# Selective scan: the row steps also make dt, B and C of the column directions, and both row sweeps run first

## Chip, cores and metric

One core of one Trainium2 chip. The metric is the device time of one launch in microseconds; before the change it is 9641.94 us, the median of 3 runs (9639.81 to 9643.63).

## What is computed

Two layers over x of shape (8, 192, 64, 64), float32. The change is in the first, a two-dimensional selective scan over four directions (k = 0: rows, 1: columns, 2: rows backwards, 3: columns backwards). Cut to what matters:

```
xn = layernorm(x); xc, z = split(in_proj_w @ xn)
xc = silu(depthwise_conv3x3(xc) + conv_b)
x_hw = xc as (D, L), rows after each other        # L = 64 * 64 = 4096
x_wh = xc transposed, columns after each other
xs = stack([x_hw, x_wh, reversed x_hw, reversed x_wh])
dts, B, C = split(x_proj_w[k] @ xs[k], [12, 16])   # 12 + 4 + 4 rows
dt = softplus(dt_proj_w[k] @ dts + dt_proj_b[k])
h = exp(dt * A) * h + dt * B * u ; y = sum_n h[n] * C[n]
y of the four directions is summed in image order, + Ds * xs
out = x + out_proj_w @ (layernorm(y) * silu(z))
```

The second layer is an attention over the 4096 positions with a residual; the change does not touch it. dts, B and C of a position are linear in xc at that position, so they do not depend on the order in which a direction walks over the image.

## The kernel before

The batch is a loop over 8 images. In one image come four stages with a barrier of all engines between them (the first two run into each other): project and convolve, scan, mix, attend. In the profile an image takes about 1206 us, of which the scan's 32 steps take about 470.

**Steps.** `run_chunks` (line 216) unrolls 32 steps per image: direction k = 0, 1, 2, 3 in turn, and in each 8 chunks of 512 positions. An odd k reads its chunk of 8 columns out of the row-ordered tiles with a stride of 64 elements between neighbours (`chunk`, line 99). `body` of every engine gets the steps before, now, next and after (two ahead), because the work of a step is spread over three steps:

- two steps ahead, PE makes the 20 rows dts, B and C (`xdbl`, lines 408 and 409, two products over the 192 channels), ACT copies them to `xd` (line 735), PE makes dt's argument from `xd` (`dtproj`, line 416), ACT does softplus in pieces (lines 745 to 761), ACT and DVE split the same 20 rows in a high and a low part in `xhl` (`copy_high`, line 741, and `low_half`, line 1096), DVE makes the softplus residue (line 1102), and SP writes the B rows to memory (line 299) and reads them back spread over all partitions (`bs`, lines 302 and 305);
- one step ahead, DVE finishes softplus (`softplus`, line 1108), POOL makes dt + relu (line 951), dt * u (`du`, line 957, which reads a chunk of u) and three products with B (`dbu`, line 966);
- in its own step, ACT makes the decays (line 768), DVE scans six tiles (line 1118) and multiplies them by C in three instructions (line 1126), which need C spread over the partitions: PE does that (`spread`, line 427, two products in fp32r for each of q = 0, 1, 2). PE then sums y with the sum so far, which it reads back from `pad0` and `pad1` (`sum_first` line 435 and 438, `sum_second` 444, `sum_rest` 451 and 454), and ACT writes the sum back (lines 773 and 777).

**Order on each engine** is written out by hand and held by semaphores. On PE a step is xdbl of the step two ahead, sum_rest of the step before, spread 1, dtproj, sum_first, spread 2, sum_second, spread 0 of the next step. On DVE it is scans and C product three times (softplus of the next step after the first), then low_half and residue of the step two ahead. PSUM: bank 0 holds xdbl's result, 1 the sum, 2 and 3 the decays, 4 and 5 the spread C, 6 and 7 softplus.

`pad0` and `pad1` hold the padded input of the convolution in the first stage and the two parts of the sum in the scan. A list LOADS of weight transfers is issued by SP once, before the first image, and everything waits for them.

Of the kernel before, what the change touches and what calls it, by code (L numbers as in the profile page):

```python
# [19 lines left out]
F32 = mybir.dt.float32  # L20
# [6 lines left out]
L = HH * WW  # L27
# [10 lines left out]
LO = 32  # L38
PW = WW + 2
# [11 lines left out]
def build(nc, nb, x, vec, w_in, w_x, w_dt, sel, fold, ident, w_out, w_att, gb, w_w, out):  # L51
# [3 lines left out]
    with ctx:  # L55
# [6 lines left out]

        pad0 = sb("pad0", [P, PW * PW])
        pad1 = sb("pad1", [P, PW * PW])
# [15 lines left out]
        wx0 = sb("wx0", [P, K * P])  # L80
        wx1 = sb("wx1", [P, K * P])
# [15 lines left out]
        Y = [pad0, pad1]  # L97
# [71 lines left out]
        rden = nc.dram_tensor("rden", [T], F32, kind="Internal").ap()  # L169
        rows = [nc.dram_tensor(f"rows{i}", [NS, T], F32, kind="Internal").ap() for i in range(2)]  # L170
# [6 lines left out]
        def barrier(eng, b, n):  # L177
# [15 lines left out]
            "xdbl_ready", "xd_ready", "xhi_ready", "xlo_ready", "dtpre_ready", "soft_ready", "res_ready", "sp_ready",  # L193
# [11 lines left out]
        LOADS = [(vecs[:, :], vec), (wx0[:, :].rearrange("p (k n) -> p k n", n=P)[:, :, 0:64], w_x[0:P].rearrange("p (k n) -> p k n", n=64)),  # L205
                 (wx1[:, :].rearrange("p (k n) -> p k n", n=P)[:, :, 0:64], w_x[P:2 * P].rearrange("p (k n) -> p k n", n=64)),
                 (wdt[0:NX + 1, :], w_dt), (foldw[:, R:P], fold), (eye[:, :], ident), (wo0[:, R:C], w_out[0:P, 0:P]), (wo0[:, 0:R], w_out[0:P, P:C]),
                 (wo1[0:R, R:C], w_out[P:C, 0:P]), (wo1[0:R, 0:R], w_out[P:C, P:C]),
                 (wa0[:, :], w_att[0:P]), (wa1[0:R, :], w_att[P:C]), (wa1[R:R + 1, 2 * O:3 * O], gb), (ww[:, :], w_w), (gate[0:64, 0, 0:12 * P], sel)]
# [6 lines left out]
        def run_chunks(eng, b, body):  # L216


            def place(k, n):
                k, n = k + n // NCH, n % NCH  # L220
                return (k, n if k < 2 else NCH - 1 - n) if 0 <= k < K else None

            for k in range(K):
                for n in range(NCH):
                    body(k, n % 2, b * G + (k * NCH + n), place(k, n - 1), place(k, n), place(k, n + 1), place(k, n + 2))
# [45 lines left out]
        def _(sp):  # L271
            sp.wait_ge(S["pads_set"], 10)
# [14 lines left out]
            with sp.Fori(0, nb) as b:  # L287
# [8 lines left out]
                def body(k, par, g, before, now, nxt, after):  # L296
                    sp.wait_ge(S["xd_ready"], g + 1)
                    sp.wait_ge(S["dbu_ready"], g * NP + 1)
                    sp.dma_start(rows[par], xd[RANK:RANK + NS, :]).then_inc(S["rows_saved"], 16)
# [3 lines left out]
                    for half in range(2):  # L303
                        part = rows[par].rearrange("(e w) t -> w e t", w=2)[half:half + 1].to_broadcast([R, 2, T])
                        sp.dma_start(bs[par][half * R:half * R + R, 2, :, :], part).then_inc(S[f"b_loaded{par}"], 16)
                run_chunks(sp, b, body)
# [40 lines left out]
        def _(pe):  # L347
# [10 lines left out]
            with pe.Fori(0, nb) as b:  # L358
# [45 lines left out]
                def xdbl(k, c, g):  # L404

                    pe.wait_ge(S["xlo_ready"], g + 1)
                    order = k % 2
                    mm(flat(ps[:, 0, :]), wx0[:, k * P:(k + 1) * P], chunk(u[:, 0], c, order), start=True, stop=False)  # L408
                    mm(flat(ps[:, 0, :]), wx1[:, k * P:(k + 1) * P], chunk(u[:, 1], c, order), start=False, stop=True)\  # L409
                        .then_inc(S["xdbl_ready"], 1)  # L410

                def dtproj(k, g):
                    pe.wait_ge(S["xd_ready"], g + 1)
                    pe.wait_ge(S["dt_ready"], g + 1)
                    for r in range(2):
                        m = mm(ps[:, 6 + r, :], wdt[:, (2 * k + r) * P:(2 * k + r + 1) * P], xd[:, :],  # L416
                               start=True, stop=True)
# [966 lines left out]
```

## Time and profile before

| what | value |
|---|---|
| median of 3 runs | 9641.94 us |
| profiled execution: its own time | 9653.1 us |
| its span, first to last instruction | 9651.3 us |
| PE busy, of the span | 9020.4 us, 93% |
| DVE busy | 7422.2 us, 77% |
| ACT busy | 6225.7 us, 65% |
| POOL busy | 3292.1 us, 34% |
| mean granted TensorE clock | 0.974 of full speed |

Times are microseconds from the span's start unless marked ns. PE is TensorE's matmul, DVE is VectorE, ACT is ScalarE, POOL is GpSimd, SP issues the transfers. L427 is line 427 of the kernel. Busy time of PE is modelled from pipelined matmuls; what its work costs is better read from the distance between the starts of rows that follow each other without a wait. One fp32 product of 128x512 shows as two matmul records, one fp32r product as one. The times here belong to the profiled execution, 11 us above the median.

### The profile page before, as it was taken

What the parts mean: (1) busy time and instruction counts of PE and PEld (TensorE: products, weight loads), DVE (VectorE), ACT (ScalarE), POOL (GpSimd) and SP (SyncE); (2) the same over time, 40 slices, a digit from 0 to 9 for tenths busy, and PEclk for the clock granted to TensorE, in tenths of its full rate; (3) what the DMA queues carried; (4) which work ended last, traced back from release to release, by engine and by line L of the source; (5) the groups of instructions that cost most, each with busy time, mean ns of one, the idle gap of its engine ahead of it and who ended that gap; (6) DMA issues with size and microseconds to landing.
All of it is one profiled execution on the core that took longest, in us unless ns stands there. A gap on an engine that the chain in (4) does not pass through costs nothing. (4 is left out here: it accounts for less than half of the span.)

```text
span 9651.3 us, 105800 instructions
## 1 busy us (share of the span) xinstructions
PE 9020.4 (93%) x27076; PEld 4814.2 (50%) x27076; DVE 7422.2 (77%) x8305; ACT 6225.7 (65%) x7692; POOL 3292.1 (34%) x1873
## 2 busy tenths in 40 slices
PE   7999989999899998999989999899998999989999
PEld 3336733367333673336733367333663336633466
DVE  6977679776797767977679776797767977679776
ACT  6765667656675566755667556675567755677555
POOL 3850038500385003850038500384003840048400
PEclk9999999999999999999999999999999999999999
DMA  2320013200132001320013200232002320023100
GB/s 66 106 71 11 12 58 106 70 11 12 58 108 68 11 12 60 110 66 10 12 63 108 66 10 12 65 106 66 10 12 65 106 66 10 12 65 110 61 10 13
DMA packets 214540, 499.71 MB, mean 52 GB/s; under 512 B 71001, under 2 KB 71993, under 8 KB 181262
## 3 DMA queue, kind: packets, MB, share of 16 engines
q1 hardware_dynamic: 214030, 494.10, 16.8%
q8 instruction: 174, 2.85, 0.1%
q14 instruction: 336, 2.75, 0.1%
HBM read 466.39 MB, written 27.38 MB: 51 GB/s over the span
## 5 line engine op out<-in xcount | busy, mean ns | idle before, releaser
L1255 DVE TENSOR_TENSOR pl<-pf,ph 128x1024 fp32r<-128x1024 f32 x1024 | 1254.0, 1225 | 1021.9 <-ACT ph L901 1014.7
L1118 DVE TENSOR_TENSOR_SCAN h<-ps,h,dbu 128x512 f32<-128x512 f32 x1536 | 1884.2, 1267 | 50.3 <-POOL dbu L966 32.6
L966 POOL TENSOR_TENSOR dbu<-bs,du 128x1024 f32<-128x1024 f32 x768 | 1799.2, 2372 | 54.1 <-POOL du L957 54.1
L901 ACT ACTIVATE ph<-pf 128x1024 fp32r<-128x1024 f32 x1024 | 1085.7, 1060 | 758.7 <-PE ps L601 758.5
L895 ACT ACTIVATE pf<-ps 128x1024 f32<-128x1024 f32 x1024 | 1050.9, 1026 | 536.3 <-PE ps L588 536.3
L921 POOL MEMSET sqb<- 64x512 f32 x16 | 8.3, 519 | 4003.4 <-issue 3998.5
L768 ACT ACTIVATE ps<-dt,negA 128x512 f32<-128x512 f32 x1536 | 1032.5, 683 | 409.1 <-DVE h L1118 401.6
L1239 DVE TENSOR_REDUCE mx<-ps 128x1 f32<-128x512 f32 x1792 | 1167.8, 683 | 78.9 <-PE ps L506 61.2
L1126 DVE TENSOR_TENSOR hc<-h,ps 128x1024 f32<-128x1024 f32 x768 | 937.4, 1221 | 198.4 <-PE ps L427 118.5
L957 POOL TENSOR_TENSOR du<-dt,u 128x512 f32<-128x512 f32 x512 | 715.0, 1419 | 647.6 <-DVE dt L1108 646.9
L951 POOL TENSOR_TENSOR dt<-dt,ze 128x1024 f32<-128x1024 f32 x256 | 605.9, 2367 | 922.4 <-ACT dt L761 922.4
L586 PE MATMUL ps<-thc,phh 97*128 97x512 f32 x2048 | 846.0, 413 | 6.8 <-ACT thc L878 6.8
L427 PE MATMUL ps<-xhl,selr 128*128 128x512 f32 x1536 | 698.8, 536 | 148.3 <-DVE hc L1126 148.3
L599 PE MATMUL ps<-ph,gth 128*97 128x512 f32 x2048 | 818.5, 400 | 11.7 <-DVE pl L1255 8.6
L587 PE MATMUL ps<-thc,phl 97*128 97x512 f32 x2048 | 815.4, 398 | 0.0
L588 PE MATMUL ps<-thc,phh 97*128 97x512 f32 x2048 | 812.8, 397 | 0.0
L601 PE MATMUL ps<-pl,gth 128*97 128x512 f32 x2048 | 810.6, 396 | 0.0
L600 PE MATMUL ps<-ph,gtl 128*97 128x512 f32 x2048 | 809.2, 395 | 0.0
L506 PE MATMUL ps<-phh,thc 96*128 96x512 f32 x1824 | 632.7, 408 | 47.3 <-POOLq L180 18.8
L416 PE MATMUL ps<-xd,wdt 128*128 128x512 f32 x1024 | 509.2, 621 | 81.8 <-DVE dt L1108 74.7
L427 PEld LDWEIGHTS ps<-xhl,selr 128*128 128x128 f32 x1536 | 267.7, 192 | 607.4 <-DVE hc L1126 395.9
L454 PE MATMUL ps<-hc,foldw 128*128 128x512 f32 x1024 | 495.1, 606 | 0.0
(188 smaller groups left out, 15369.5 us busy)
## 6 DMA issues: line engine op xcount, KB each, us to landing
bs<-rows SPq DMA_DIRECT2D x256, 1024.0 KB, 5.2
bs<-rows SPq DMA_DIRECT2D x512, 256.0 KB, 6.1
xa<-in_x SPq DMA_DIRECT2D x130, 256.0 KB, 2.9
xb<-in_x SPq DMA_DIRECT2D x130, 128.0 KB, 3.0
out<-fa SPq DMA_DIRECT2D x64, 256.0 KB, 2.0
rdb<-rden SPq DMA_DIRECT2D x56, 192.0 KB, 3.4
out<-fa SPq DMA_DIRECT2D x64, 128.0 KB, 2.3
rows<-xd SPq DMA_DIRECT2D x256, 8.0 KB
```

The source lines that it names most:

```text
L427: m = mm(ps[:, 4 + e, :], selr[:, j * P:(j + 1) * P], xhl[par][:, :], start=True, stop=True)
L586: mm(dst, kk, thc[par][0][:, :], start=True, stop=False)
L587: mm(dst, phl[:, m * P:(m + 1) * P], thc[par][0][:, :], start=False, stop=False)
L599: mm(dst, gth[:, m, :], ph[:, mp % 2, e, :], start=(m == 0), stop=False)
L768: A(ps[:, 2 + e, :], dt[par][:, 0 if j < NS else 1, :], ACT.Exp, scale=negA[:, k * NT + j:k * NT + j + 1]).then_inc(S["dA_ready"], 1)
L895: A(pf[:, mp % 2, :, :], ps[:, 2 * (mp % 2):2 * (mp % 2) + 2, :], ACT.Exp)\
L901: A(ph[:, mp % 2, :, :], pf[:, mp % 2, :, :], ACT.Copy).then_inc(S["ph_ready"], 1)
L966: pool.tensor_tensor(dbu[:, q, :, :], bs[par][:, q, :, :], du[:, r:r + 1, :].to_broadcast([P, 2, T]), ALU.mult).then_inc(S["dbu_ready"], 1)
L1118: dve.tensor_tensor_scan(h[:, j, ::step], ps[:, 2 + e, ::step], dbu[:, q, e, ::step], h[:, j, end:end + 1], ALU.mult, ALU.add)\
L1126: TT(hc[:, q, :, :], h[:, 2 * q:2 * q + 2, :], ps[:, 4:6, :], ALU.mult).then_inc(S["hc_ready"], 1)
L1239: dve.tensor_reduce(mx[:, t, m:m + 1], ps[:, 5 + j % 2, :], AX.X, ALU.max)\
L1255: TT(pl[:, mp % 2, :, :], pf[:, mp % 2, :, :], ph[:, mp % 2, :, :].bitcast(F32), ALU.subtract)\
```

## The change

- The order of the sweeps is k = 0, 2, 1, 3, so the 16 row steps come before the 16 column steps.
- The x_proj product of a row step now has more columns of weight: besides the 20 rows of its own direction it gives C of directions 1 and 3 (in two copies, at partitions 20 to 27 and 84 to 91) and dts and B of directions 1 and 3 (from partitions 32 and 48). Time per product depends on the 512 positions, which stay.
- In 8 of the 16 row steps (STORE), which cover the 8 row chunks once, ACT also writes all of the product's result to a new tile `xsf`, transposed to column order (`store_xs`; `xsf` lies over `pad1`), and SP writes the C rows, high and low, from `xhl` to a new tensor `ct` in memory, in row order.
- Column steps have no xdbl, no copy to `xd`, no copy_high and no low_half. dtproj reads `xsf`, SP takes the B rows from `xsf`, and SP reads the C rows from `ct` into `xhl`, in pieces of 8 elements (64 rows of the image by 8 columns, for 4 partitions, two such transfers per step). `spread` then reads `xhl` with a stride of 8 elements (32 bytes), in column order.
- copy_high and low_half of the row steps cover 128 and 64 partitions instead of 64 and 32.
- The second part of the sum moves from `pad1` to `gate[:, 1]`.
- LOADS grows from 23 to 58 transfers, because the weights are put together column by column.

```diff
+ORDER = (0, 2, 1, 3)
+EV = 2 * NCH
+STORE = (3, 5, 7, 9, 11, 13, 14, 15)
+ONE = NX + 2 * NS
...
+        for w, rows_ in ((wx0, slice(0, P)), (wx1, slice(P, 2 * P))):
+            for s, k in enumerate((0, 2)):
+                at = s * P
+                LOADS += [(w[:, at:at + NX], w_x[rows_, 64 * k:64 * k + NX]), (w[:, at + R + RANK + NS:at + R + NX], w_x[rows_, 64 * k + RANK + NS:64 * k + NX])]
+                for i, kk in enumerate((1, 3)):
+                    c_of, m = w_x[rows_, 64 * kk + RANK + NS:64 * kk + NX], at + NX + NS * i
+                    LOADS += [(w[:, m:m + NS], c_of), (w[:, R + m:R + m + NS], c_of),
+                              (w[:, at + LO + 16 * i:at + LO + 16 * i + 16], w_x[rows_, 64 * kk:64 * kk + 16])]
...
@@ SP, body
+                    if at < EV:
+                        sp.wait_ge(S["xd_ready"], b * EV + (at + 1))
+                        src = xd[RANK:RANK + NS, :]
+                    else:
...
+                        src = xsf[m:m + NS, bass.ds(c * T, T)]
                     sp.wait_ge(S["dbu_ready"], g * NP + 1)
...
+                    if at in STORE:
+                        sp.wait_ge(S["xlo_ready"], b * EV + (at + 2))
+                        for m, row in ((0, NX), (2 * NS, R + NX)):
+                            sp.dma_start(ct[m:m + 2 * NS, c * T:(c + 1) * T], xhl[par][row:row + 2 * NS, :].bitcast(F32))\
+                                .then_inc(S[f"c_stored{par}"], 16)
+                    if at >= EV:
...
+                        sp.wait_ge(S["cbc_ready"], g * NP + 1)
+                        for m, row in ((0, RANK + NS), (2 * NS, R + RANK + NS)):
+                            m += NS * (k // 2)
+                            src = ct[m:m + NS, :].rearrange("r (h w) -> r h w", w=WW)[:, :, c * RPC:(c + 1) * RPC]
+                            dst = xhl[par][row:row + NS, :].bitcast(F32).rearrange("p (h w) -> p h w", w=RPC)
+                            sp.dma_start(dst, src).then_inc(S[f"c_loaded{par}"], 16)
...
@@ PE
+                    src = xd[:, :] if at < EV else xsf[:, c * T:(c + 1) * T]
...
-                        m = mm(ps[:, 4 + e, :], selr[:, j * P:(j + 1) * P], xhl[par][:, :], start=True, stop=True)
+                        src = flat(xhl[at % 2][:, :]) if at < EV else xhl[at % 2][:, :].rearrange("p (h w) -> p w h", w=RPC)
+                        m = mm(flat(ps[:, 4 + e, :]), selr[:, j * P:(j + 1) * P], src, start=True, stop=True)
...
-                    if after:
-                        xdbl(*after, g + 2)
+                    if after and at + 2 < EV:
+                        xdbl(*after, b * EV + (at + 2))
...
@@ ACT
+                def store_xs(c):
+
+                    A(chunk(xsf, c, 1), flat(ps[:, 0, :]), ACT.Identity, bias=eye[:, ONE:ONE + 1]).then_inc(S["xs_ready"], 1)
...
                         soft_exp(g + 2)
-                        copy_high(par, g + 2)
+                        if at + 2 in STORE:
+                            store_xs(after[1])
+                        if at + 2 < EV:
+                            copy_high(at + 2, g + 2)
...
@@ DVE
                     if after:
-                        low_half(par, g + 2)
+                        if at + 2 < EV:
+                            low_half(at + 2)
                         residue(g + 2)
```

How this moves instructions is seen best at two places.

PE, a column step in the middle of a sweep, before (pad is `pad1` in L451 and `pad0` in L435, hc the scanned tiles times C):

```order
L408 MATMUL ps<-u,wx 128x512 [waits xlo_ready]
L409 MATMUL ps<-u,wx 128x512
L451 MATMUL ps<-pad,eye 128x512 [waits y0_added]
L452 REGISTER_ALU
L454 MATMUL ps<-hc,foldw 128x512 [waits hc_ready]
L454 MATMUL ps<-hc,foldw 128x512
L422 REGISTER_ALU
L427 MATMUL ps<-xhl,selr 128x512 [waits hc_ready]
L427 MATMUL ps<-xhl,selr 128x512
L416 MATMUL ps<-xd,wdt 128x512 [waits dt_ready,xd_ready]
L416 MATMUL ps<-xd,wdt 128x512
```

and the same stretch of a column step now:

```order
L502 MATMUL ps<-gate,eye 128x512 [waits y0_added]
L503 REGISTER_ALU
L505 MATMUL ps<-hc,foldw 128x512 [waits hc_ready]
L505 MATMUL ps<-hc,foldw 128x512
L470 REGISTER_ALU
L478 MATMUL ps<-xhl,selr 128x512 [waits hc_ready]
L478 MATMUL ps<-xhl,selr 128x512
L462 REGISTER_ALU
L465 MATMUL ps<-xsf,wdt 128x512 [waits dt_ready]
L465 MATMUL ps<-xsf,wdt 128x512
```

The two xdbl products are gone. The rest is the same in number and order, but L478 reads `xhl` with its stride, which these rows do not show.

ACT, a row step whose chunk two ahead is stored, now (from softplus's exponential, L808, to the sum's first part, L829):

```order
L808 ACTIVATE za<-za 128x1024 [waits soft_ready]
L790 ACTIVATE xsf<-ps,eye 128x8x64
L794 ISA
L797 ACTIVATE xhl<-ps 128x512 [waits cbc_ready]
L811 REGISTER_ALU
L812 ACTIVATE ps<-za 128x1024 [waits soft_ready]
L816 REGISTER_ALU
L817 ACTIVATE dt<-za 128x1024 [waits du_ready]
L823 ISA [waits dt_ready]
L824 ACTIVATE ps<-dt,negA 128x512 [waits scan_link]
```

L790 is new, and stands ahead of copy_high (L797), softplus's last two parts and the decay (L824) that the next step's first scan waits for.

## Rows read from the trace of the kernel before

**Rows 1.** The page's part 1: busy us (share of the span) xinstructions.
```profile
PE 9020.4 (93%) x27076; PEld 4814.2 (50%) x27076; DVE 7422.2 (77%) x8305; ACT 6225.7 (65%) x7692; POOL 3292.1 (34%) x1873
```
**Rows 2.** Timeline of DVE, first scans of steps 8, 16 and 24: start, us, what.
```profile
1491.20 2.46 DVE L1118 TENSOR_TENSOR_SCAN h<-ps,h,dbu 128x512 f32<-128x512 f32 x2 [0.33 <-DVE h L1145]
...
1611.86 2.46 DVE L1118 TENSOR_TENSOR_SCAN h<-ps,h,dbu 128x512 f32<-128x512 f32 x2 [0.34 <-POOL dbu L966]
...
1727.24 2.46 DVE L1118 TENSOR_TENSOR_SCAN h<-ps,h,dbu 128x512 f32<-128x512 f32 x2 [0.33 <-DVE h L1145]
```
**Rows 3.** Timeline of DVE, the end of a row step.
```profile
1652.98 0.68 DVE L1096 TENSOR_TENSOR xhl<-ps,xhl 32x512 fp32r<-32x512 f32 x1
1653.70 1.23 DVE L1102 SCALAR_TENSOR_TENSOR ps<-ps,za 128x1024 f32<-128x1024 f32 x1
1654.96 1.28 DVE L1118 TENSOR_TENSOR_SCAN h<-ps,h,dbu 128x512 f32<-128x512 f32 x1
```
**Rows 4.** Timeline of DVE, a column step.
```profile
1520.95 2.46 DVE L1118 TENSOR_TENSOR_SCAN h<-ps,h,dbu 128x512 f32<-128x512 f32 x2
...
1524.67 1.22 DVE L1108 SCALAR_TENSOR_TENSOR dt<-ps,dt 128x1024 f32<-128x1024 f32 x1
...
1533.09 1.22 DVE L1126 TENSOR_TENSOR hc<-h,ps 128x1024 f32<-128x1024 f32 x1 [1.12 <-PE ps L427]
...
1536.32 1.28 DVE L1118 TENSOR_TENSOR_SCAN h<-ps,h,dbu 128x512 f32<-128x512 f32 x1
```
**Rows 5.** Timeline of PE, the same column step.
```profile
1521.49 1.90 PE L409 MATMUL ps<-u,wx 128*128 128x512 f32 x2
1523.21 1.90 PE L451 MATMUL ps<-pad,eye 128*128 128x512 f32 x2
1524.93 1.90 PE L454 MATMUL ps<-hc,foldw 128*128 128x512 f32 x4
...
1527.12 1.88 PE L416 MATMUL ps<-xd,wdt 128*128 128x512 f32 x4
...
1530.54 1.90 PE L438 MATMUL ps<-hc,eye 128*128 128x512 f32 x4
...
1534.36 0.73 PE L427 MATMUL ps<-xhl,selr 128*128 128x512 f32 x2
1535.08 1.96 PE L408 MATMUL ps<-u,wx 128*128 128x512 f32 x2
```
**Rows 6.** Timeline of PE, a row step.
```profile
1640.31 1.02 PE L409 MATMUL ps<-u,wx 128*128 128x512 f32 x2
1641.17 1.02 PE L451 MATMUL ps<-pad,eye 128*128 128x512 f32 x2
```
**Rows 7.** Timeline of ACT: line 773 in a column step and in a row step.
```profile
1536.55 1.03 ACT L773 ACTIVATE pad<-ps 128x512 f32<-128x512 f32 x1
...
1654.65 0.58 ACT L773 ACTIVATE pad<-ps 128x512 f32<-128x512 f32 x1
```
**Rows 8.** Timeline of POOL, a column step.
```profile
1526.06 3.03 POOL L957 TENSOR_TENSOR du<-dt,u 128x512 f32<-128x512 f32 x2 [2.72 <-DVE dt L1108]
1529.26 7.03 POOL L966 TENSOR_TENSOR dbu<-bs,du 128x1024 f32<-128x1024 f32 x3 [0.17 <-POOL du L957]
1536.25 2.36 POOL L951 TENSOR_TENSOR dt<-dt,ze 128x1024 f32<-128x1024 f32 x1
```
**Rows 9.** Timeline of ACT, the end of a row step.
```profile
1651.53 1.01 ACT L756 ACTIVATE ps<-za 128x1024 f32<-128x1024 f32 x1
...
1653.42 1.29 ACT L768 ACTIVATE ps<-dt,negA 128x512 f32<-128x512 f32 x2
```
**Rows 10.** Timeline of SP's issues, the first and the last of LOADS.
```profile
4.59 0.41 SPq L274 DMA_DIRECT2D vecs<-in_vec  x1
...
12.61 4.53 SPq L274 DMA_DIRECT2D win<-in_w_in  x8
```
**Rows 11.** DMA issues: names, engine, op, count, KB each, median us to landing.
```profile
thc<-nmr SPq DMA_DIRECT2D x224, 0.5 KB, 2.0
```

More of the change, by code:

```diff
@@ L63, in build @@
         pad0 = sb("pad0", [P, PW * PW])
+        with ExitStack() as at_pad1:
+            xsf = sb("xsf", [P, L], where=at_pad1)
         pad1 = sb("pad1", [P, PW * PW])
@@ L216, in run_chunks, with place @@
         def run_chunks(eng, b, body):
[L219 to L225, printed above, removed]
+            def place(at):
+                if not 0 <= at < G:
+                    return None
+                k, n = ORDER[at // NCH], at % NCH
+                return k, n if k < 2 else NCH - 1 - n
+            for at in range(G):
+                body(at, at % 2, b * G + at, place(at - 1), place(at), place(at + 1), place(at + 2))
         def run_project(eng, step, early=None):
@@ L271, in _ @@
         def _(sp):
[L272 removed]
+            sp.wait_ge(S["pads_set"], 11)
             for dst, src in LOADS:
@@ L294, in _, with body @@
                 sp.sem_inc(mark, 1)
-                def body(k, par, g, before, now, nxt, after):
-                    sp.wait_ge(S["xd_ready"], g + 1)
+                def body(at, par, g, before, now, nxt, after):
+                    k, c = now
+                    if at < EV:
+                        sp.wait_ge(S["xd_ready"], b * EV + (at + 1))
+                        src = xd[RANK:RANK + NS, :]
+                    else:
+                        if at == EV:
+                            sp.wait_ge(S["xs_ready"], b * NCH + NCH)
+                        m = LO + 16 * (k // 2) + RANK
+                        src = xsf[m:m + NS, bass.ds(c * T, T)]
                     sp.wait_ge(S["dbu_ready"], g * NP + 1)
-                    sp.dma_start(rows[par], xd[RANK:RANK + NS, :]).then_inc(S["rows_saved"], 16)
+                    sp.dma_start(rows[par], src).then_inc(S["rows_saved"], 16)
                     sp.wait_ge(S["rows_saved"], g * 16 + 32)
@@ L402, in step, with xdbl @@
                         remainder(c - 2)
[L404 to L409, printed above, removed]
-                        .then_inc(S["xdbl_ready"], 1)
-                def dtproj(k, g):
-                    pe.wait_ge(S["xd_ready"], g + 1)
+                def xdbl(k, c, e):
+                    pe.wait_ge(S["xlo_ready"], e + 1)
+                    w = slice((k // 2) * P, (k // 2) * P + P)
+                    mm(ps[:, 0, :], wx0[:, w], u[:, 0, c * T:(c + 1) * T], start=True, stop=False)
+                    mm(ps[:, 0, :], wx1[:, w], u[:, 1, c * T:(c + 1) * T], start=False, stop=True)\
+                        .then_inc(S["xdbl_ready"], 1)
@@ L776, in add_y1, with body @@
                     act.wait_ge(S["summed"], g * NP + 6)
-                    A(chunk(pad1, c, k % 2, R, P), flat(ps[R:P, 1, :]), ACT.Copy).then_inc(S["y1_added"], 1)
-                def body(k, par, g, before, now, nxt, after):
+                    A(chunk(gate[:, 1], c, k % 2, R, P), flat(ps[R:P, 1, :]), ACT.Copy).then_inc(S["y1_added"], 1)
+                def body(at, par, g, before, now, nxt, after):
                     s = g * NP
+                    k = now[0]
                     decay(k, 1, 0, s + 1, par, g)
-                    if after:
-                        copy_xd(g + 2)
+                    if after and at + 2 < EV:
+                        copy_xd(at + 2, g + 2)
                     decay(k, 1, 1, s + 1, par, g)
@@ L967, in drive, with body @@
                                        du[:, r:r + 1, :].to_broadcast([P, 2, T]), ALU.mult).then_inc(S["dbu_ready"], 1)
-                def body(k, par, g, before, now, nxt, after):
+                def body(at, par, g, before, now, nxt, after):
                     if nxt:
@@ L1126, in times_c, with body @@
                     TT(hc[:, q, :, :], h[:, 2 * q:2 * q + 2, :], ps[:, 4:6, :], ALU.mult).then_inc(S["hc_ready"], 1)
-                def body(k, par, g, before, now, nxt, after):
+                def body(at, par, g, before, now, nxt, after):
                     for q in range(NP):
                         s = g * NP + q
-                        scans(k, q, s)
+                        scans(now[0], q, s)
                         times_c(q, s)
@@ L1151, in early @@
                     if n == 1:
-                        low_half(0, g_0)
+                        low_half(0)
                     elif n == 2:
```

102 lines of the change are left out of this document (58 added, 44 removed).

## The prediction

> **What bounds the kernel now.** I read the page's shares first, then how far the scan's steps lie apart, then DVE and PE inside one step of each kind. The shares [rows 1] say little: PE is busy 93% and DVE 77% of the span, as means over stages with different limits. The change lies in the scan, in what is loaded before the first image, and nowhere else, so the length of a step decides. The first scans of steps 8, 16 and 24 [rows 2] give a column sweep (8 to 16) 1611.86 - 1491.20 = 120.7 us and a row sweep (16 to 24) 115.4 us. Two limits stand behind that.
>
> In a row step DVE is the bound. At its end low_half starts at 1652.98, residue at 1653.70 and the next scan at 1654.96 with nothing idle between [rows 3]; the distance from low_half to residue, 0.72 us, is what a step without low_half saves where DVE is the bound.
>
> In most column steps PE is the bound. The step lasts 1536.32 - 1520.95 = 15.37 us, and DVE's last product with C stands idle for 1.12 us for the spread of line 427 [rows 4]. The reason is in how PE reads. In the column step the product of line 409 takes 1523.21 - 1521.49 = 1.72 us and that of line 451 takes 1.72 us [rows 5]; in a row step the same line 409 takes 1641.17 - 1640.31 = 0.86 us [rows 6]. Four products per column step read their 512 positions 256 bytes apart (xdbl's two, and the sum so far twice) and cost double. ACT shows the same when it writes that way: line 773 takes 1.03 us in a column step, 0.58 in a row step [rows 7]. One spread product, fp32r and read in order, is short: from line 454 to line 416 PE needs 2.19 us [rows 5] for two fp32 products (1.72) and two spread products, so 0.235 us for one.
>
> **PE's budget of a column step.** Line 408 of the next step stands at 1535.08, so that of this one stood 15.37 us before, at 1519.71, and xdbl lasts until line 451 at 1523.21 [rows 5]: 3.50 us. The six spread products take 0.47 + 0.47 + 0.72 (1535.08 - 1534.36, with a wait) = 1.66, and the rest 10.2. The change takes xdbl out: 11.9 us are left, and DVE would be the bound again. But it also makes the six spread products read 32 bytes apart, which no row of before shows for fp32r. The bounds: at nothing, 0.235 us each. At most, the 0.86 us in which one pass of a product is read 256 bytes apart (an fp32 product is two passes, 1.72 us). In between, a doubling to 0.45, as the fp32 product doubles. I take 0.86. A pass of 512 in 0.86 us is 1.67 ns for an element; ACT, another engine, comes to about the same: its own pace is (1.01 - 0.58) / 512 = 0.84 ns [rows 7, 9], and the strided write adds (1.03 - 0.58) / 512 = 0.88, so 1.72. Two engines that both stop at about 1.7 ns for an element point to a limit of the memory per access, and then fp32r, which asks faster, falls to it by more than a factor of two. The Trainium skill (SBUF — State Buffer, Door 1: The DMA port swizzle) has a rule that speaks against the change: SBUF works in lines of 16 bytes, and an access that goes to a new line each time pays. By that rule 32 bytes cost as much as 256, and no spread product stays at 0.235; no row of before shows a 32-byte step.
>
> So a column step costs PE 10.2 + 6 x 0.86 = 15.4 us. With nothing lost between, and a little for waits, I take **15.5 us** for all column steps. DVE would need only the row steps' 115.4 / 8 = 14.4 less 0.72, or 13.7.
>
> **The sum for one image.**
> - First column sweep: 7 x 15.5, and 14.6 for its first step, whose sum_rest still belongs to a row step and reads in order (0.86 less): 123.1 against 120.7 us, **+2.4**.
> - Second column sweep: the same +2.4. But its last step had no xdbl before, since nothing lies two steps ahead, and gives nothing up for its two spreads (q = 1, 2): 4 x (0.86 - 0.235) = 2.5 more, **+4.9** together.
> - The last two row steps lose low_half, since the steps two ahead are column steps: 2 x 0.72, **-1.4**.
> - Eight row steps gain store_xs on ACT, 1.03 us by rows 7. It stands ahead of the softplus part of line 756, which then ends at 1651.53 + 1.0 + 1.0 = 1653.5, in time for the residue at 1653.70 [rows 3, 9]. The decay would end at 1653.42 + 1.0 + 0.69 = 1655.1, against a scan that wants to start at 1654.96: 0.2 us late, 8 times, **+1.6**. Bounds: 0 (the slack holds) and 1.0 each.
> - Copies of 128 and 64 partitions instead of 64 and 32 are taken as free, since low_half on 32 partitions takes 0.68 us for 512 elements [rows 3] and line 773 on all 128 no more, 0.58 [rows 7]: the length of a row counts.
>
> Together +7.5 us per image, **+60** for eight.
>
> **Once, at the start:** 23 transfers are issued from 4.59 to 17.14 us [rows 10], 0.55 us each, and everything waits for them. 35 more make **+19** (bounds 10 and 30, as they are smaller but cut in more pieces).
>
> **What I cost at nothing.** SP's two transfers of C per column step are issued when spread 2 of the step two back is through, so their cover is more than the whole step between, about 15 us. The nearest row is a transfer of 128 pieces of 4 bytes, which lands in 2.0 us [rows 11]; 256 pieces each for two transfers may be 4 to 8 us. SP also does them after its B rows of that step, whose own need is a step later, so a wait there delays nobody until it passes about 12 us. The eight stores of C wait on SP for low_half, one step before their buffer is written again. The three sweep changes stay three, with a pause of about 0.33 us each [rows 2]; at the one in PE's own time it hides. POOL and ACT do the same as before or less in column steps. In the other stages only addresses change.
>
> Sum: +60 + 19 = +79 on the profiled 9653.1 us, or 9732; that execution lies 11 us above the median, so the forecast for the median is 9642 + 80 = **9722 us**.
>
> **Rivals.**
> 1. *The strided fp32r read costs little or only doubles (0.24 to 0.45 us a product).* PE then needs 10.2 + 2.7 = 12.9 us or less, and xdbl's removal pays. Other loops set the step: POOL goes from softplus's end (1524.67 + 1.22) over du and dbu to the end of line 951 at 1538.61 [rows 4, 8], then 1.22 us of softplus again, 13.95 us in all; with a little for the handovers I take 14.1. A column sweep is 112.8 us against 120.7, so -7.9 for the first; for the second, whose last steps were short already, -6. With -1.4 + 1.6 this is -13.7 per image, -110 for eight, and +19 at the start: about **9551 us**, faster. For it: the factor of two that rows 5 and 6 show could be one of two cycles for one, relative to the engine's own pace, since ACT at nearly the same pace cannot tell a factor from a limit; 32 bytes are also a smaller step than 256. Against it: the agreement in absolute time. The side changes at 0.76 us a product: each 0.01 us is worth 6 x 16 x 8 x 0.01 = 7.7 us, and 79 / 7.7 is 10 of them.
> 2. *In between:* 0.7 to 0.8 us a product, so 14.4 to 15.0 us a column step with PE still the bound: 123 to 46 us below the forecast, **9600 to 9676 us**.
> 3. *The C transfers land late.* Pieces of 32 bytes could take far longer than the ones in rows 11. If landing took 20 us, each column step would wait some 4 us: 16 x 8 x 4 = +500 us, **10200 us**. Against it: 128 pieces in 2.0 us, and a cover of a step. The Trainium skill (DMA: Bandwidth & Descriptors, Specifications) puts full rate at 512 bytes and more, which these pieces miss by far, but gives no latency for them.
> 4. *PE has bubbles too* (the back-written sum comes 0.3 us before PE wants it): 15.8 to 16 us a step, **9760 to 9790**.
>
> **How the numbers follow.** The forecast 0.55, with its own range 9685 to 9765 (steps of 15.3 to 15.7 us, start 10 to 30, stores 0 to 64 at their bounds but most likely near 13). Rival 1: 0.29, from 9530 to 9590. Rival 2: 0.06. Rival 3: 0.02. Rival 4: 0.08. A measurement here tells 0.2% (19 us) from no change. Faster 0.31 (rival 1 and a third of rival 2), same 0.03 (half of rival 2), slower 0.66. The range that holds 8 in 10 has to take in both sides: 9540 to 9765.
>
> **What would show it.** Right: spread rows in a column step at 0.86 us from start to start, 15.4 to 15.6 us between steps, PE without a gap there and DVE idle for about 1.8 us a step behind the spread of q = 2; the row steps at 14.4 to 14.6; the first matmul some 19 us later in the span. Wrong: a spread pair of less than 1.2 us in a column step, with DVE or POOL as the last to release; an idle PE that waits for the C transfers; or row steps that grow by more than 0.5 us.

## The result, and the profile after

The changed kernel takes 9578.33 us (median, 9572.66 to 9585.77) against 9641.67 us: ratio 0.9933, interval 0.9921 to 0.9946. It is faster by 63 us, and the forecast of 9722 us was on the wrong side. Of the cases written down, rival 1 (9551 us, with a range of its own from 9530 to 9590) is the one that holds it. The profiled execution of the changed kernel has a span of 9583.9 us against 9651.3, 67 us less. From the scans' starts in the two traces: the first scan comes 16.5 us later (186.6 against 170.1), the eight scan stages together take 87.6 us less (3652.7 against 3740.3, first to last scan), and all the rest, 3.7 us more.

Part 1 of the page of after, which answers to [rows 1]:

```profile
PE 8813.6 (92%) x26564; PEld 4729.1 (49%) x26564; DVE 7318.6 (76%) x8161; ACT 6190.6 (65%) x7500; POOL 3294.3 (34%) x1874
```

The shares hardly move; again a single step tells more. DVE in a column step of after (timeline: start, us, what, idle before and its releaser), which answers to [rows 4]:

```profile
1656.03 2.45 DVE L1175 TENSOR_TENSOR_SCAN h<-ps,h,dbu 128x512 f32<-128x512 f32 x2
...
1667.82 1.22 DVE L1183 TENSOR_TENSOR hc<-h,ps 128x1024 f32<-128x1024 f32 x1 [0.77 <-PE ps L478]
1668.96 1.23 DVE L1159 SCALAR_TENSOR_TENSOR ps<-ps,za 128x1024 f32<-128x1024 f32 x1
1670.09 1.27 DVE L1175 TENSOR_TENSOR_SCAN h<-ps,h,dbu 128x512 f32<-128x512 f32 x1
```

The step is 1670.09 - 1656.03 = 14.06 us, not 15.5. DVE still waits for the spread of q = 2, for 0.77 us. PE in the same step, which answers to [rows 5]:

```profile
1657.07 1.97 PE L502 MATMUL ps<-gate,eye 128*128 128x512 f32 x2 [0.93 <-ACT pad L829]
1658.86 1.90 PE L505 MATMUL ps<-hc,foldw 128*128 128x512 f32 x4
1660.19 1.43 PE L478 MATMUL ps<-xhl,selr 128*128 128x512 f32 x2
1661.44 1.90 PE L465 MATMUL ps<-xsf,wdt 128*128 128x512 f32 x4
```

From line 505 to line 465 PE needs 1661.44 - 1658.86 = 2.58 us. The two fp32 products in it take 1.72, so the two strided spread products take 0.86 together, **0.43 us each**; I had taken 0.86 each. Line 502 does what line 451 did before; new is its wait of some 0.9 us in every step for ACT's write-back of the sum. PE is no longer the bound by its work alone.

What the step's length hangs on can be read from PE and ACT together. PE starts sum_rest at 1657.07 and works without a gap through spread 1 and dtproj (line 465). ACT takes dtproj's first result at 1663.37 and works without a gap through softplus, the two decays and the write-back, and PE's next sum_rest starts as that ends (timelines of ACT and of PE):

```profile
1663.37 1.03 ACT L801 ACTIVATE za<-ps 128x1024 f32<-128x1024 f32 x1 [0.48 <-PE ps L465]
...
1668.82 1.29 ACT L824 ACTIVATE ps<-dt,negA 128x512 f32<-128x512 f32 x2
1670.04 1.03 ACT L829 ACTIVATE pad<-ps 128x512 f32<-128x512 f32 x1
```
```profile
1671.13 1.11 PE L502 MATMUL ps<-gate,eye 128*128 128x512 f32 x1 [0.85 <-ACT pad L829]
```

1671.13 - 1657.07 = 14.06 us: a closed loop over PE and ACT. The experiments below test it.

Not every step is that short. In image 1 the column steps of after read 13.93, 15.50, 14.05, 14.06, 15.48, 14.05, ... from scan to scan. In the long ones PE is slow. The same four passes of line 505 in the long step before (timeline), and the stretch around them (windows: PE, PEld, DVE, ACT, POOL busy, then the granted clock, DMA share, GB/s):

```profile
1629.31 3.34 PE L505 MATMUL ps<-hc,foldw 128*128 128x512 f32 x4
```
```profile
1629.00:1632.00 3.00, 3.00 (x6) 1.13 (x4) 2.72 (x3) 0.66 (x1) 1.50 (x2) 0.50 0.52 214
```

3.34 us instead of 1.90, and a granted clock of 0.50 (1.2 GHz instead of 2.4): the clock fell for a short stretch. The records of after have 30 such stretches in the column steps of the eight images (steps 16 to 30, counted from 0), three or four per image, and each costs its step 1.0 to 1.6 us. Before has 8 in its column steps, one per image in step 30, none elsewhere but in the first step of each image, where both kernels have one. After has 10 more in steps 14 and 15, two row steps in which PE has no xdbl either.

The start, SP's issues of after (answers to [rows 10]):

```profile
11.48 15.12 SPq L296 DMA_DIRECT2D wx<-in_w_x  x32
...
28.64 4.34 SPq L296 DMA_DIRECT2D win<-in_w_in  x8
```

The 58 transfers are issued from 4.85 to 32.98 us, 0.49 us each.

### The profile page after: what moved, and what is told of

Read it like the earlier page. It is cut to its first block and busy times, and to the rows that moved or that the text cites. A ratio compares the mean times of both kernels' runs of the same rounds, so it can differ in the third digit from the quotient of the medians.

```text
span 9583.9 us, 104556 instructions
## 1 busy us (share of the span) xinstructions
PE 8813.6 (92%) x26564; PEld 4729.1 (49%) x26564; DVE 7318.6 (76%) x8161; ACT 6190.6 (65%) x7500; POOL 3294.3 (34%) x1874
## 5 line engine op out<-in xcount | busy, mean ns | idle before, releaser
L824 ACT ACTIVATE ps<-dt,negA 128x512 f32<-128x512 f32 x1536 | 1038.3, 688 | 494.5 <-DVE h L1175 494.1
L478 PE MATMUL ps<-xhl,selr 128*128 128x512 f32 x1536 | 847.8, 639 | 147.7 <-DVE hc L1183 147.5
L478 PEld LDWEIGHTS ps<-xhl,selr 128*128 128x128 f32 x1536 | 271.3, 196 | 631.0 <-DVE hc L1183 370.5
L505 PE MATMUL ps<-hc,foldw 128*128 128x512 f32 x1024 | 548.1, 662 | 0.0
L489 PE MATMUL ps<-hc,eye 128*128 128x512 f32 x1024 | 484.3, 595 | 0.0
```

The source lines that it names most:

```text
L478: m = mm(flat(ps[:, 4 + e, :]), selr[:, j * P:(j + 1) * P], src, start=True, stop=True)
L824: A(ps[:, 2 + e, :], dt[par][:, 0 if j < NS else 1, :], ACT.Exp, scale=negA[:, k * NT + j:k * NT + j + 1]).then_inc(S["dA_ready"], 1)
```

## Experiments

All ran beside runs of the kernel before, in three groups in which its medians are 9640.92, 9641.11 and 9643.61 us. Where a text below counts stretches at half clock, it counts those in the column steps 16 to 30 of all eight images in the profiled execution; after has 30.

| run | median us | ratio to before, interval |
|---|---|---|
| after | 9578.33 | 0.9933, 0.9921 to 0.9946 |
| e1_inorder | 9544.62 | 0.9898, 0.9882 to 0.9915 |
| e2_strides | 9590.16 (one run) | |
| e3_order | 9661.41 | 1.0020, 1.001 to 1.003 |
| e4_busy | 9559.64 | 0.9914, 0.9897 to 0.9931 |
| e6_b_xdbl_inorder | 9571.21 | 0.9928, 0.9908 to 0.9948 |
| e8_low_half | 9661.06 | 1.0021, 1.0011 to 1.0031 |
| e9_early_y0 | 9532.78 | 0.9891, 0.9874 to 0.9907 |
| e11_du_inorder | 9577.39 | 0.9949, 0.9922 to 0.9975 |
| e7_two_queues | 9559.71 (one run) | |
| e12_early_two | 9525.80 | 0.9873, 0.9857 to 0.9890 |
| e10_all | 9537.64 | 0.9893, 0.9877 to 0.9910 |
| e13_early_inorder | 9534.51 | 0.9884, 0.9868 to 0.9901 |

**The price of a strided fp32r read (e2_strides).**

```diff
-                        src = flat(xhl[at % 2][:, :]) if at < EV else xhl[at % 2][:, :].rearrange("p (h w) -> p w h", w=RPC)
-                        m = mm(flat(ps[:, 4 + e, :]), selr[:, j * P:(j + 1) * P], src, start=True, stop=True)
+                        view = lambda t, n: t.rearrange("p (a b) -> p b a", b=n)
+                        src, dst = flat(xhl[at % 2][:, :]), flat(ps[:, 4 + e, :])
+                        if at >= EV:
+                            n = (2, 4, 64)[q]
+                            src = view(xhl[at % 2][:, :], n)
+                            dst = ps[:, 4 + e, :].rearrange("p (b a) -> p b a", b=n)
+                        m = mm(dst, selr[:, j * P:(j + 1) * P], src, start=True, stop=True)
```

> The changed kernel, but in the column steps spread q=0 reads xhl with a step of 8 bytes, q=1 with 16 bytes, q=2 with 256 bytes (C in the wrong order). Theory A (fp32r at full clock costs 0.22 us in order and twice that, 0.43 us, wherever the step leaves the line): 0.22 at 8 bytes, 0.43 at 16 and at 256. Rival B (there is a limit in time per access of 1.67 ns, and 32 bytes is cheaper only because it is a smaller step): 0.86 us a product at 256 bytes. The page's lines of 16 bytes with two hits enough say 0.22 at 8 bytes.

PE of e2_strides in a column step (timeline); the spread of 256 bytes is the one behind line 494, that of 8 bytes the one behind line 500, that of 16 bytes the one behind line 510:

```profile
1668.18 1.90 PE L494 MATMUL ps<-hc,eye 128*128 128x512 f32 x4
1669.51 1.54 PE L483 MATMUL ps<-xhl,selr 128*128 128x512 f32 x2
1670.87 1.90 PE L500 MATMUL ps<-hc,eye 128*128 128x512 f32 x4
1672.59 1.15 PE L483 MATMUL ps<-xhl,selr 128*128 128x512 f32 x2
...
1676.24 1.90 PE L510 MATMUL ps<-hc,foldw 128*128 128x512 f32 x4
1677.57 1.48 PE L483 MATMUL ps<-xhl,selr 128*128 128x512 f32 x2
1678.88 1.90 PE L465 MATMUL ps<-xsf,wdt 128*128 128x512 f32 x4
```

At 256 bytes: 1670.87 - 1668.18 - 1.72 = 0.97 us for two, 0.49 each. At 16 bytes: 1678.88 - 1676.24 - 1.72 = 0.92, 0.46 each. After has 0.43 at 32 bytes, before 0.235 in order. There is no 0.86 at any step, so the limit of 1.67 ns per access, on which my price stood, does not exist for these reads; the stride about doubles what the product takes in order, for fp32 (0.86 to 1.72) and for fp32r alike. The 8-byte step did not come out as either theory had it: its pair shows 1.15 us where the in-order pair at that place shows 0.73 [rows 5, line 427], a little above the 1.10 that the 32-byte pair shows there in after. So it pays about as much as 32 bytes. The Trainium skill (SBUF — State Buffer, Door 1: The DMA port swizzle) puts the border at 16-byte lines and says that two hits per line are enough; 8-byte steps have two hits and paid here. Its other half, that each access to a new line pays, agrees: 16, 32 and 256 bytes all did.

**What the strided read costs the kernel (e1_inorder).** Spreads read `xhl` in order, so C belongs to other positions.

```diff
-                        src = flat(xhl[at % 2][:, :]) if at < EV else xhl[at % 2][:, :].rearrange("p (h w) -> p w h", w=RPC)
+                        src = flat(xhl[at % 2][:, :])
```

> The changed kernel, but spread reads xhl in order in the column steps too, so C comes out in the wrong order of positions. After the change a column step takes 14.05 us, a spread product 0.43 us, and PE waits 0.93 us for the write-back of the sum (add_y0). Theory A (the column step is a loop over PE and ACT: sum_rest, spread 1, dtproj, softplus, decays, add_y0): one spread pair lies in the loop, so 0.43 us less, but POOL's loop of 13.95 us is next, so 13.95 to 14.0 us and 5 to 15 us in all. Rival B (POOL's loop alone sets 14.05): no change in the step, 14.05. Theory C (the granted clock falls because PE has idle time in these steps): spreads that end sooner leave PE more idle, so more stretches at half clock than the 30 in the column steps of after, and the kernel gets slower than 9578, by up to 30 us. Rival D (the clock falls for another reason, such as the strided reads): fewer or none, 9535 to 9550.

34 us less: more than theory A and rival B said, and in rival D's range, but by another way than D's. The steps are 13.6 to 14.1 us, and DVE waits no longer for PE but for POOL. Waits of DVE over steps in the middle of image 1, first after, then e1_inorder (us in total, times, longest):

```profile
DVE hc L1183 <- PE ps L478: 10.2, 11, 1.5
```
```profile
DVE dt L1165 <- POOL dt L1011: 4.9, 9, 0.6
DVE hc L1183 <- PE ps L478: 1.5, 2, 1.1
```

Both of theory A's loops can be seen: the shortest steps, 13.60 to 13.66, are the loop over PE and ACT less the 0.43 us, and the others wait for POOL. The clock still falls, 26 times instead of 30, though PE waits longer (1.54 us at line 502). That speaks against theory C in its plain form (more idle, more falls), and hardly for D: the spreads are not strided here, and 26 falls are left. All column steps together take 28 us less than in after (1688.8 against 1717.0 us).

**The clock (e4_busy).** One more product, whose result nobody reads, ahead of the wait for the write-back; busy is true for the sum_rest that PE does in steps 17 to 31.

```diff
+                    if busy:
+                        mm(ps[:, 0, :], eye[:, :], wdt[:, 0:T], start=True, stop=True)
                     pe.wait_ge(S["y0_added"], g + 2)
...
-                        sum_rest(*before, g - 1)
+                        sum_rest(*before, g - 1, at > EV)
```

> The changed kernel with one more fp32 product of 128x512 (0.86 us, its result is never read) on PE ahead of sum_rest in column steps 17 to 31, where PE now waits 0.93 us for add_y0. Theory C (the clock falls because PE has this idle time): the product fills the wait, the stretches at half clock in the column steps go from 30 to near none, the steps of 15.5 to 15.7 us become 14.05, and the kernel gains about 30 x 1.5 = 45 us: 9530 to 9545. Rival D (the clock falls for another reason): no fewer stretches, and 9578 or some us more, as the product delays sum_rest a little.

The long steps are gone: 14.04 to 14.12 us each (a sweep change 14.5). There are 7 stretches instead of 30, all in the first column step, ahead of the extra product; in steps 17 to 30, where it stands, there is none and after has 26. The granted clock over steps 16 to 30 of image 1, first after, then e4_busy:

```profile
1612.56:1813.76 201.20, 188.50 (x364) 69.69 (x364) 183.66 (x156) 149.97 (x183) 173.44 (x85) 0.97 0.37 112
```
```profile
1612.18:1810.12 197.94, 196.44 (x390) 73.73 (x391) 183.65 (x155) 151.17 (x184) 172.88 (x85) 0.99 0.37 114
```

So without PE's pause at that place the clock does not fall there. The gain is 19 us and not 45: in the profiles the column steps give back 34 us (1683.1 against 1717.0 us for eight images), and other stages, where the clock also moves, take some.

**Shortening the pause (e9_early_y0).**

```diff
                         decay(nxt[0], 0, 0, s + 3, 1 - par, g + 1)
+                        if at >= EV:
+                            add_y0(*now, g)
                         decay(nxt[0], 0, 1, s + 3, 1 - par, g + 1)
-                    add_y0(*now, g)
+                    if not nxt or at < EV:
+                        add_y0(*now, g)
```

> The changed kernel, but in column steps ACT writes the sum back (add_y0) between the two decays of the next step and not behind both, so 0.6 us earlier; PE waits 0.93 us for it now. Theory A (chain over PE and ACT at 14.05, POOL's loop at 13.95 right below): the step goes to 13.95 to 14.0, 5 to 15 us in all, 9563 to 9573. Rival B (DVE's scan then waits for the second decay): 14.2 us or more, 9590. On the clock I expect no change: PE is as idle as before.

45 us less, although the steps stay at 14.02 to 14.14. What went are the long ones: 3 stretches instead of 30, all in step 16, and in image 1 none, so that the clock over its steps 16 to 30 is 1.00. In the profiled executions 39 of the 52 us between the spans lie in the column steps (1678.1 against 1717.0).

```profile
1604.76:1801.81 197.05, 187.56 (x364) 66.02 (x364) 183.81 (x156) 149.38 (x182) 173.06 (x85) 1.00 0.37 114
```

PE idles 9.5 us here against 12.7 in after, which is not much less. PE's waits in the same stretch, first after, then e9_early_y0, show what else changed: one wait of 0.87 us on average per step became two of about 0.33.

```profile
PE ps L502 <- ACT pad L829: 12.2, 14, 0.9
```
```profile
PE ps L502 <- ACT pad L829: 4.6, 14, 0.7
PE ps L465 <- DVE dt L1168: 4.3, 13, 0.4
```

I had expected 5 to 15 us here and no change of the clock. The size was wrong through the clock. That the steps did not get shorter, with the loop over PE and ACT 0.6 us shorter, means that another loop stands right behind it: DVE's softplus now waits for POOL's dt + relu in 12 of 14 steps (3.1 us in all; in after 2 times, 0.5 us).

**The loops at 14.05 (e11_du_inorder, e8_low_half).** POOL reads u in row order in column steps (du of wrong positions):

```diff
-                        m = pool.tensor_tensor(flat(du[:, r, :]), flat(dt[par][:, r, :]), chunk(u[:, r], c, k % 2), ALU.mult)
+                        m = pool.tensor_tensor(flat(du[:, r, :]), flat(dt[par][:, r, :]), chunk(u[:, r], c, 0), ALU.mult)
```

> The changed kernel, but POOL reads u in order for du in the column steps (wrong positions), 2.50 instead of 3.03 us for two. Theory A (the chain over PE and ACT sets 14.05): no change of the step, 9578 within 6. Rival B (POOL's loop, softplus, du, dbu, dt + relu, sets it): 13.65 us, where DVE is the bound, 0.4 x 15 x 8 = 48 us less, 9530.

Theory A: 9577 against 9578 us, steps of 14.04. POOL's loop does not set the step of after. (One of the ten runs took 9700.28 us, at a granted clock of 0.924; the median does not feel it, the interval does.)

e8_low_half puts an instruction of low_half's size back on DVE:

```diff
                         if at + 2 < EV:
                             low_half(at + 2)
+                        else:
+                            TT(xd[R:P, :], ps[R:P, 0, :], wdt[R:P, 0:T], ALU.subtract)
```

> The changed kernel with a DVE instruction of low_half's size (64 partitions of 512, into a part of xd that nothing reads) where low_half stood in the column steps, 0.72 us a step. Theory A (in the column steps the chain over PE and ACT is the bound, and DVE has slack, 0.77 us idle at the spread of q = 2): the step goes from 14.05 to DVE's 14.37, not by 0.72 but by about 0.35, x 15 x 8 = 40 us, so 9610 to 9625. Rival B (DVE is the bound after all): 14.75 us a step, 9660.

Rival B's number, 9661 us: the instruction costs 83 us, more than the whole change won. A step is 14.69 us (the step's first scan starts at 1667.50 in the timeline, the next step's at 1682.19), 0.64 more than in after, and the clock falls 40 times instead of 30. DVE in that step, and PE's dtproj and next sum_rest:

```profile
1671.22 1.22 DVE L1165 SCALAR_TENSOR_TENSOR dt<-ps,dt 128x1024 f32<-128x1024 f32 x1
...
1678.96 1.22 DVE L1183 TENSOR_TENSOR hc<-h,ps 128x1024 f32<-128x1024 f32 x1 [0.45 <-PE ps L478]
1680.21 0.69 DVE L1198 TENSOR_TENSOR xd<-ps,wdt 64x512 f32<-64x512 f32 x1
1680.92 1.23 DVE L1159 SCALAR_TENSOR_TENSOR ps<-ps,za 128x1024 f32<-128x1024 f32 x1
1682.19 2.46 DVE L1175 TENSOR_TENSOR_SCAN h<-ps,h,dbu 128x512 f32<-128x512 f32 x2
```
```profile
1672.49 1.98 PE L465 MATMUL ps<-xsf,wdt 128*128 128x512 f32 x4
...
1682.26 1.97 PE L502 MATMUL ps<-gate,eye 128*128 128x512 f32 x2 [0.84 <-ACT pad L829]
```

Two things show. From the start of the C product to the next scan it is 3.23 us here and 2.27 in after (1670.09 - 1667.82): the instruction costs 0.96 us, not the 0.72 between two starts, as its neighbours start later too. And a loop other than that of after now sets the step. It goes from DVE's scan to the end of softplus (1667.50 to 1671.22 + 1.22 = 1672.44), over PE's dtproj, sum_first and spread 2 to DVE's last C product (1672.49 to 1678.96), and over the extra instruction and the residue to the next scan (1682.19). Without the 0.96 us it would be 13.73 us, 0.32 below the loop over PE and ACT, and 0.96 - 0.32 is the 0.64 by which the step grew. DVE's wait of 0.77 us in after was therefore no slack of that size: what DVE does late in a step delays PE's dtproj of the next. So in the column steps of after three loops lie close together: PE and ACT at 14.05, POOL's right behind it (14.02 to 14.14 where e9_early_y0 leaves it alone), and DVE with PE at 13.7. This order is worked out from the rows and agrees with e1, e8, e9, e11 and e13; no run takes away PE and ACT's loop and POOL's at the same time.

**The order of sweeps alone (e3_order).**

```diff
-            for k in range(K):
-                for n in range(NCH):
...
+                k, n = (0, 2, 1, 3)[at // NCH], at % NCH
+                return k, n if k < 2 else NCH - 1 - n
```

> The kernel before with the order of sweeps 0, 2, 1, 3 and nothing else. Theory: the order itself costs nothing; each column sweep keeps its five steps of 15.37 us. 9642 within 5 us. Rival: the order brings or takes some of the difference, since the last row step now goes to a column step once and not three times between kinds: up to 2 us per image, 9626 to 9658.

It costs 20 us, a little more than the rival's 16. 13 of them can be seen in the scan stages of the two profiled executions (3684.7 against 3671.3 us); where the rest lies is open. DVE's first scans of steps 23 and 24, and of 25, in image 1:

```profile
1715.75 2.46 DVE L1119 TENSOR_TENSOR_SCAN h<-ps,h,dbu 128x512 f32<-128x512 f32 x2
```
```profile
1731.57 2.46 DVE L1119 TENSOR_TENSOR_SCAN h<-ps,h,dbu 128x512 f32<-128x512 f32 x2 [0.34 <-ACT ps L769]
```
```profile
1746.52 2.46 DVE L1119 TENSOR_TENSOR_SCAN h<-ps,h,dbu 128x512 f32<-128x512 f32 x2
```

15.82 and 14.95 us. In the order of before every column sweep begins and ends next to a row sweep, where xdbl or sum_rest of the neighbour read in order and PE catches up (14.37 and 14.5 us). Two column sweeps behind each other lose that. So the second half of what the title says costs something where PE is the bound. In after PE alone is not the bound: the three steps around the change between the column sweeps are 14.06, 14.53 and 13.74 us in image 1, 0.2 us more together than three other steps.

**Where the gain comes from (e6_b_xdbl_inorder).** The kernel before, xdbl reading u in row order in all directions (dt, B and C of wrong positions).

```diff
-                    order = k % 2
+                    order = 0
```

> The kernel before, but xdbl reads u in row order in the column steps too (so dt, B and C of the columns are those of other positions). Theory A (the ten steps of 15.37 us per image stand on PE alone, through the strided reads): PE needs 1.72 us less, DVE becomes the bound, all steps 14.37 us, so 10 x 1.0 x 8 = 80 us less, 9560. Rival B (as PE has then more idle time, its clock falls now and then): 9570 to 9600 with stretches at half clock in the column steps that before had 27 us of them in all.

Theory A: 70 us less by the medians, 81 in the scan stages of the profiled executions (3590.7 against 3671.3 us), with column steps of 14.50 instead of 15.37. Rival B's falls did not come: 5 stretches, all in step 30, where before has 8. The strided reads of xdbl alone cost before as much as the whole change wins.

**The start (e7_two_queues) and the combinations (e12_early_two, e10_all, e13_early_inorder).**

```diff
-            for dst, src in LOADS:
+            for dst, src in LOADS[0::2]:
                 sp.dma_start(dst, src).then_inc(s_load, 16)
...
+            for dst, src in LOADS[1::2]:
+                act.dma_start(dst, src).then_inc(s_load, 16)
```

> The changed kernel with every second transfer of LOADS issued by ACT instead of SP. Theory: the 16.5 us by which the first scan starts later than before (186.6 against 170.1 us) are the issues of 35 more transfers at 0.47 us each on one queue; two queues halve 58 x 0.49, so the first scan is 12 to 14 us earlier, at about 173. Rival: the transfers themselves are slow and two queues do not help: 187.

The first scan starts at 172.9 us, as the theory said. PE's first matmul, before, after and with two queues (the last from e12_early_two):

```profile
18.64 1.44 PE L350 MATMUL ps<-win,vecs 128*1 128x384 f32 x2 [18.64 <-DMA win<-in_w_in]
```
```profile
34.50 1.44 PE L395 MATMUL ps<-win,vecs 128*1 128x384 f32 x2 [34.50 <-DMA win<-in_w_in]
```
```profile
21.27 1.44 PE L395 MATMUL ps<-win,vecs 128*1 128x384 f32 x2 [21.27 <-DMA win<-in_w_in]
```

> The changed kernel with add_y0 between the decays in the column steps and with LOADS on two queues: 9533 less 13 at the start, so 9515 to 9525. No stretches at half clock in the middle of the column steps.

9525.8 us, 0.8 above the range. Its first scan comes 15.5 us earlier than that of e9_early_y0, its median is only 7 lower: its runs go from 9510.64 to 9531.44, and its interval overlaps with that of e9_early_y0. In the profiled executions the clock falls in step 16 in six images here and in three there, and in steps 14 and 15 twelve times against four; steps 17 to 30 have none in either, as expected.

> As the kernel with early add_y0 and two queues, with the extra product of 0.86 us ahead of sum_rest besides. Theory: the wait it fills has gone (0.4 us left), so the product now delays sum_rest by up to 0.45 us and the step goes from 14.05 to 14.1 to 14.5: 5 to 50 us slower than the kernel without it. Rival: it still helps, through the few stretches at half clock that are left at the start of the column steps: up to 10 us faster.

The median is 12 us above e12_early_two, with intervals that overlap. That lies in the 5 to 50 us that I gave, but not for my reason: the steps stay at 14.03 to 14.16 in the trace, so the product delays nothing that matters. It gains nothing; whether it costs anything the runs do not settle.

> The changed kernel with add_y0 between the decays and with spread reading xhl in order (C in the wrong order). It prices the strided read of C where the clock does not fall. Theory A (three chains lie at 14.0: DVE's scan, C product and softplus into PE's dtproj, sum_first and spread; PE and ACT; POOL): the strided read is in the first two only, POOL's 13.95 stays, so at most 0.1 us a step, 9520 to 9533. Rival B (POOL's loop has slack when PE is earlier): 13.65 a step, 9490. If the clock falls again because PE idles more, up to 40 us slower than 9533.

9534.5 against 9532.8 us, steps mostly of 14.02 to 14.12, and DVE waits for POOL's dt + relu. Theory A in the main (1.5 us above its range): with the write-back early, the strided read of C costs the kernel nothing. The clock does fall again, 14 times against 3, 11 of them in steps 17 to 30, but it costs little: a step of 14.64 us is followed by one of 13.5, as PE has room to catch up. PE is busy 173.69 us of 196.39 here, far less than in after, and it falls half as often: the sum of idle time alone does not decide.

```profile
1603.63:1800.02 196.39, 173.69 (x364) 66.79 (x364) 184.27 (x155) 147.81 (x182) 172.49 (x85) 0.99 0.37 115
```

## Why the prediction was wrong

The step that failed is the price of the strided spread product: "I take 0.86". It measures 0.43. All the rest of the forecast's sign hung on it, as the text itself said (the side changes at 0.76). The argument behind it was that PE and ACT both stop at about 1.7 ns per element, and so a limit in time. But both engines also have about the same pace in order (0.84 ns per element: PE (0.86 / 2) / 512 us, ACT as in the text), so the agreement could not tell a limit from a factor. The text named that under rival 1 and then gave it 0.29. The rule of the Trainium skill (SBUF — State Buffer, Door 1: The DMA port swizzle) that I set beside it says that a penalty exists, and gives no size; it could not support 0.86 against 0.45. With the price halved a column step is not 15.5 us on PE but 14.05 on a loop over PE and ACT.

By the steps of the forecast:
- *Column steps are bound by PE through strided reads:* right for the kernel before. e6_b_xdbl_inorder, reading xdbl in order and nothing else, gives 70 us.
- *PE's budget of 10.2 us beside the spreads:* right within 0.3; with 6 x 0.43 it makes 12.8 us, and a step of after less PE's wait is 14.06 - 0.93 = 13.1.
- *DVE would need 13.7 us:* 13.41, since low_half costs 0.96 us and not 0.72: the row steps with it take 14.37. In after a row step without it (step 14, image 1) goes from 1585.14 to 1598.55:

```profile
1585.14 2.46 DVE L1175 TENSOR_TENSOR_SCAN h<-ps,h,dbu 128x512 f32<-128x512 f32 x2
...
1598.55 1.27 DVE L1175 TENSOR_TENSOR_SCAN h<-ps,h,dbu 128x512 f32<-128x512 f32 x1
```

- *store_xs, +1.6 us per image:* about right. Steps with it are 14.48 to 14.51 us, those without 14.38, and one (step 5) is 14.87: some 1.3 us per image.
- *The start, +19 us:* 16.5.
- *The transfers of C are hidden:* right. No engine's list of waits over steps 16 to 30 of image 1 has them.
- *The sweep order costs nothing but the pauses:* on the kernel before it costs 20 us (e3_order). The sum had the neighbour's part for the first column step (14.6) but did not ask what before gained from three changes between kinds. In after, where PE alone is not the bound, nearly none of it shows.
- *The clock:* the forecast has no term for it. Its falls cost after about 40 us.

Rival 1 had the mechanism: 14.1 us a step against 14.05. Its loop was not the first, though: it named POOL's, and e11_du_inorder, with POOL 0.5 us a step faster, stays at 14.04. POOL's loop is the next one behind that over PE and ACT, and there, in e9_early_y0, its 14.1 is right. That 9578 us lie as near as 27 us to its 9551 is in part luck. The falls of the clock, which no case had, cost about 40 us: the column steps of the eight images take 1717.0 us in after and 1678.1 in e9_early_y0, where all but 3 of the 30 falls are gone and the other steps are as long. With them gone the kernel takes 9533 us, 18 below rival 1.

How the 63 us are made up can't be added from single edits, each against its own base: xdbl's strided reads out of the column steps, -70; low_half out, -83, a part of it by fewer falls of the clock; order of sweeps, +20 where PE is the bound; falls of the clock, +45; start, +16.5. The first two are two bounds of the same steps. That taking low_half out is worth nothing before xdbl has gone follows from DVE's idle 1.12 us in a column step of before, and was not run.

## What to carry to other kernels

Where two engines agree in time on a penalty, first check whether they also agree without it; a factor and a limit can be told apart only by a case with another pace, and if the trace has none, the two prices are two forecasts of near equal chance. When a change lifts a bound, write the chain that comes next as a closed loop over all engines, with each instruction's full effect on its neighbours. And look at what one pause of a matmul engine per step does to its clock: moving one small write-back by 0.6 us was worth 45 us, where the change itself won 63. A wait that one engine shows is not slack of that size if the engine it waits for hangs on it in turn.

The lowest median here, not clear of that of e9_early_y0, is that of the changed kernel with add_y0 between the two decays and the first loads on two queues, at 9525.80 us, ratio 0.9873 (0.9857 to 0.9890) to the kernel before.

## What the runs showed of the hardware that I had not expected

- An fp32r product of 128x512 takes 0.235 us read in order and 0.43 to 0.49 us at steps of 16, 32 and 256 bytes. At 8 bytes it pays as well.
- TensorE at full clock in a loop of 14.05 us with one pause of about 0.9 us in it had its granted clock halved (1.2 GHz instead of 2.4) for a short stretch three or four times in 215 us. In steps 17 to 30 of the eight images that is 26 times; with the pause filled (e4_busy) or split in two of about 0.33 us (e9_early_y0) it is never. The total idle share does not order the cases (falls in all images, clock and busy time in image 1): 26 falls in steps 16 to 30 and 0.97 at 175.31 us busy of 199.07 (e1_inorder), 14 and 0.99 at 173.69 of 196.39 (e13_early_inorder), 30 and 0.97 at 188.50 of 201.20 (after). What decides stays open.
- In e8_low_half the steps are longer (14.69 us) and the clock fell more often, 40 times, seven times in the column steps of four of the images; the cost of its extra instruction holds some of that.
- A DVE instruction of 0.69 us on 64 partitions (64 to 127), set between two that work on all 128 and read PSUM, cost 0.96 us of DVE's time. Why its neighbours start later no run shows.
